# Layer 2: attention scores and their tanh moved into the step that makes their operand, next to the aggregation products

## The chip, the cores and the metric

The kernel runs on one core of one Trainium2 chip. A core has five engines that work side by side and wait for each other through semaphores: TensorE (PE, matrix products, written into the eight 2 KB PSUM banks of each partition), VectorE (DVE), ScalarE (ACT), GpSimd (POOL) and SyncE (SP, which only issues transfers here). The metric is the device time of one launch in microseconds (us). The kernel before takes 1876.17 us, the median of three runs from 1875.2 to 1877.63 us.

## The reference

128 graphs of 64 nodes, 256 features each, go through four layers of the form x + layer(relu(layernorm(x))). The change touches the third, called layer 2, a graph attention with 4 heads and a gate. For one graph with h the normalised input:

```python
Wh = einsum('bni,hoi->bhno', h, W) + bW          # 4 heads, 256 features each
e = einsum('bhno,hop->bhnp', Wh, attn)
scores = einsum('bhnp,bhmp->bhnm', e, Wh)
A_mat = tanh(where(adj, scores, 0.0))
hp = relu(einsum('bhnm,bhmo->bhno', A_mat, Wh))
ha = cat_of_heads(hp) @ A_w.T
hf = h @ fc_w.T
coeff = sigmoid(hf @ g1_w.T + ha @ g2_w.T + gbias)
return hf * coeff + ha * (1.0 - coeff)
```

## The kernel before

The tokens are cut into 32 groups of 256 (four graphs, held as two pairs of 128 partitions). A layer is a software pipeline over groups, written out by hand for every engine as one function `step(g)`; `run_steps` calls it for g = 0 to 34, the middle ones in a loop of two. In step g of layer 2 an engine works on several groups at once: `gn` = g is being normalised, `b1` = g-1 gets its dense products, `c2` = g-2 its attention, and `e` = g-3 its final blend and store. Nothing reorders instructions: each engine takes them as `step` writes them. `after(engine, signal, group, k)` is a wait, `known(...)` is one that is emitted only outside the loop, because inside another wait implies it.

The weights are folded so that the scores of a head need one dense product: **G** (`product_g(h)`, 12 matmuls of 128x256 for each of 4 heads, each in three parts because operands are split in a high and a low half, `mm3`, L188 to L190) gives `gT`, written out of PSUM with a bias by VectorE (L1789). The **scores** are then `gT` against the transposed input `ln.hT` (L1968, 32 small products for a group; the trace lists 64). A row term is added as the bias of the **tanh** on ScalarE (L1743, result `th`), and it comes from four extra columns of **Wh**, the last four of 1028 (`WC`). Wh (`product_wh(i)`) is made in six units `UNITS = (pair, first column, width)`; VectorE writes each to `wh` (L1799). Two units, those that begin at column 768, are 260 wide and hold the four bias columns.

`th` times the adjacency matrix is `a`, the heads 0 and 1 by GpSimd (L1713) and 2 and 3 by VectorE (L1832). The **hp** products (L1937, the trace lists 128 small matmuls) multiply `a` with `wh`; ScalarE takes the relu (L1733, `cat_hi`), VectorE the low half (L1806, `cat_lo`). Then come the `ha` products with `aw` (96 matmuls), `hf` and the gate products with `sq`. After the gate product ScalarE takes a tanh (L1771), VectorE blends in three operations (`diff` L1814, `part` L1817, `yT` L1822), TensorE transposes `yT` into bank 0 (L1982) and VectorE adds the residual to give `y` (L1844).

TensorE's order in a step before: scores of c2; G products of heads 0 and 1 of b1; transposes of `yT` of e; G products 2 and 3; hp of c2; six Wh units of b1; transposes of the normalised input of gn (L307, bank 0); `ha`; `hf`; gate. The scores use bank 4, the G products banks 1, 2, 3 and 1.

VectorE's order in a step before: `diff`, `part`, `yT` of e; layernorm statistics (L262); `a` of c2; the rest of the statistics (L269, L274); `gT` 0 and 1; `y`; `gT` 2 and 3; `ln_shift` (L288); three `cat_lo`, `wh` unit 0, the fourth `cat_lo`, the other `wh` units; then the low halves of the next operands.

Of the kernel before, what the change touches and what calls it, by code (L numbers as in the profile page):

```python
# [16 lines left out]
P = 128  # L17
S = 64
D = 256
KC = D // P  # L20
PAIRS = 2
# [75 lines left out]
def known(eng, signal, g, k=None, apart=None):  # L97

    if g.reg is None:
        after(eng, signal, g, k, apart)
# [1496 lines left out]
def graph_attention_layer(core, ln, x_dram, y_dram, adjT, weights, loaded_early, next_weights):  # L1600
# [6 lines left out]
    H = 4  # L1607
    CH = H * KC
    WC = H * D + H
    UNITS = ((0, 0, 512), (1, 0, 512), (0, 512, 256), (0, 768, WC - 768), (1, 512, 256), (1, 768, WC - 768))  # L1610
    graph_attention_setup(core, weights, loaded_early, next_weights)
    ctx = ExitStack()
    with ctx:  # L1613
# [39 lines left out]
                          "blend_steps", "proj_in_psum", "y_ready"]  # L1653
        B_HT = B_YT = 0
        B_G, B_WH, B_HF = (1, 2, 3, 1), (2, 3, 1, 2, 3, 1), 2
        B_GATE, B_S = 3, 4
        B_HP, B_HA = ((5, 6), (4, 7)), (7, 5)
        HEADS_OF_POOL, HEADS_OF_DVE = slice(0, 2), slice(2, H)
        halves = lambda bank: ps[:, bank, :].rearrange("p (c t) -> p c t", c=KC)
# [5 lines left out]
        def first_products(g):  # L1665


            return g.reg is None and g.c == 1
# [56 lines left out]
        @block.scalar  # L1725
        def _(act):
            def step(g):
                gn = ln.group(g)
                c2, b1 = g.back(2), g.back(1)

                def round_hp(i):
                    after(act, hp_in_psum, c2, i + 1)
                    nc.scalar.activation(in_cat(cat_hi, i), of_two_heads(i), ACT.Relu).then_inc(cat_hi_ready.sem, 1)  # L1733

                if c2.exists(groups):
                    known(act, a_pool_ready, c2.back(1))
                    known(act, a_dve_ready, c2.back(1))
                    after(act, wh_ready, c2)
                    after(act, scores_in_psum, c2)
                    for h in range(H):  # L1740
                        for p in range(PAIRS):
                            col = (p * H + h) * S
                            last = nc.scalar.activation(th[:, p, h], ps[:, B_S, col:col + S], ACT.Tanh,  # L1743
                                                        bias=wh[:, p, H * D + h:H * D + h + 1], scale=1.0)
                    last.then_inc(th_ready.sem, 1)
                if c2.exists(groups):
                    known(act, ha_in_psum, c2.back(1))
                    for i in range(H):
                        round_hp(i)
                if gn is not None:  # L1750
                    ln.apply(act, gn)
                if gn is not None:
                    known(act, scores_in_psum, gn.back(2))
                    ln.evacuate_hi(act, gn, B_HT)
                if c2.exists(groups):
                    known(act, gate_in_psum, c2.back(1))
                    for c in range(KC):
                        after(act, ha_in_psum, c2, c + 1)
                        nc.scalar.activation(ha_hi[:, c], ha(c), ACT.Copy).then_inc(ha_hi_ready.sem, 1)
                if b1.exists(groups):  # L1760
                    after(act, hf_in_psum, b1)
                    known(act, gate_in_psum, b1.back(2))
                    known(act, blend_steps, b1.back(2), 1)
                    nc.scalar.activation(hf_hi[:, b1.slot], halves(B_HF), ACT.Copy)
                    nc.scalar.activation(hf[:, b1.slot], halves(B_HF), ACT.Copy).then_inc(hf_hi_ready.sem, 1)
                if c2.exists(groups):

                    after(act, gate_in_psum, c2)
                    known(act, blend_steps, c2.back(1), 2)
                    for c in range(KC):  # L1770
                        last = nc.scalar.activation(gate[:, c], ps[:, B_GATE, c * TOK:(c + 1) * TOK], ACT.Tanh,  # L1771
                                                    bias=half_gbias[:, c:c + 1], scale=0.5)
                    last.then_inc(gate_ready.sem, 1)
                if first_products(g):
                    next_weights.split_hi(act)

            run_steps(act, step, groups, 2)

        @block.vector
        def _(dve):  # L1780
            def step(g):
# [10 lines left out]
                def evacuate_wh(i):  # L1792
                    p, c0, n = UNITS[i]
                    after(dve, wh_in_psum, b1, i + 1)
                    if i == 0:
                        known(dve, hp_in_psum, b1.back(1), 2)
                    if i == 2:
                        known(dve, hp_in_psum, b1.back(1))
                    nc.vector.tensor_tensor(wh[:, p, c0:c0 + n], ps[:, B_WH[i], 0:n], wh_bias[:, c0:c0 + n],  # L1799
                                            ALU.add).then_inc(wh_ready.sem, 1)  # L1800

# [81 lines left out]
        def _(pe):  # L1883
            def step(g):
# [35 lines left out]
                def product_hp():  # L1920
# [7 lines left out]
                    for h in range(H):  # L1928
# [10 lines left out]
                        if h % 2 == 1:  # L1939
                            for b in range(2):  # L1940
                                last[b].then_inc(hp_in_psum.sem, 1)

                def product_wh(i):
                    p, c0, n = UNITS[i]

# [7 lines left out]
                                       lambda t: t[:, c, p * P:(p + 1) * P], lambda t: t[:, c, c0 + k:c0 + k + w])  # L1953
                    last.then_inc(wh_in_psum.sem, 1)

                if c2.exists(groups):
                    u = c2.slot
                    known(pe, g_ready, c2, apart=core)
                    if first_products(g.back(1)):
                        pe.wait_ge(next_weights.made.sem, next_weights.SMALL_MADE)  # L1960
                    known(pe, th_ready, c2.back(1), apart=core)
                    for p in range(PAIRS):
                        for h in range(H):
                            col = (p * H + h) * S
                            for c in range(KC):
                                for b in range(2):
                                    toks = slice(p * P + b * S, p * P + (b + 1) * S)
                                    last = nc.tensor.matmul(ps[b * S:(b + 1) * S, B_S, col:col + S], gT[:, h, c, toks],  # L1968
                                                            ln.hT[:, u, c, toks], start=c == 0, stop=c == KC - 1,
                                                            skip_group_check=True)  # L1970
                    last.then_inc(scores_in_psum.sem, 1)
                if b1.exists(groups):
                    known(pe, ln.hT_hi_ready, b1)
                    after(pe, ln.hT_lo_ready, b1)
# [10 lines left out]
                if b1.exists(groups):  # L1985
                    product_g(2)
                    product_g(3)
                if c2.exists(groups):
                    known(pe, wh_ready, c2)
                    after(pe, a_dve_ready, c2, apart=core)  # L1990
                    after(pe, a_pool_ready, c2, apart=core)
                    product_hp()
                if b1.exists(groups):
                    for i in range(6):
                        product_wh(i)
                if gn is not None:
                    known(pe, y_ready, gn.back(3))
                    ln.transpose(pe, gn, B_HT)
                if c2.exists(groups):
                    after(pe, cat_lo_ready, c2)  # L2000
# [201 lines left out]
```

## Time and profile before

| | |
|---|---|
| median of 3 runs | 1876.17 us |
| profiled execution, its own time | 1874.63 us |
| its span | 1872.8 us |
| PE busy | 1813.7 us (97% of the span) |
| DVE busy | 1270.2 us (68%) |
| ACT busy | 896.9 us (48%) |
| POOL busy | 683.9 us (37%) |
| first and last score product of layer 2 | 676.9 us and 1479.8 us |

A timeline row gives the start and the duration in us, the engine, the line of the program, the operation, the tiles (written <- read), the shapes and how many instructions are merged in the row; in brackets the idle time before it and what ended it. Matmuls overlap: one of 128x256 lasts 0.28 us in the trace, and the next starts 0.11 us after it. PEclk is the granted TensorE clock as a share of full speed (2.4 GHz; 0.5 is 1.2 GHz).

### The profile page before, as it was taken

Reading aid. Unit: us, or ns where it says so; the run is one execution under the profiler, and the core shown is the slowest. Engines: PE = TensorE matmul, PEld = TensorE weight load, DVE = VectorE, ACT = ScalarE, POOL = GpSimd, SP = SyncE. Lnnn points to the kernel's source line nnn. Section 1 sums busy time; section 2 is a strip of 40 time slices with the busy share of each in tenths; the row PEclk is TensorE's granted clock in tenths of the full one; section 3 lists DMA queues with packets and bytes.
Section 4 is the critical chain, followed back from the end, with each engine's and each line's share of the span. In section 5 each row is a group of like instructions: output and inputs, shape, how many; then the busy total and the mean of one; then the engine's idle time right before and its main releaser. Section 6 shows DMA issues by size and latency. Waiting matters only on the chain. (4 is left out here: it accounts for less than half of the span.)

```text
span 1872.8 us, 74709 instructions
## 1 busy us (share of the span) xinstructions
PE 1813.7 (97%) x31152; PEld 1728.8 (92%) x31152; DVE 1270.2 (68%) x2887; ACT 896.9 (48%) x1997; POOL 683.9 (37%) x872
## 2 busy tenths in 40 slices
PE   7999999799999899999999999999999889999997
PEld 7899999699999799999999999999999889999997
DVE  6777777577777545555555555565555569999997
ACT  6777777566666523333333333333333335555554
POOL 3556665334343200000000000000000068999897
PEclk9999999999999999999999999999999999999999
DMA  3323223353333211101111011110111012222222
GB/s 109 88 74 86 81 73 86 111 151 91 97 91 98 89 30 37 35 26 29 34 34 34 23 29 34 34 34 23 34 29 34 19 48 78 69 69 80 74 69 64
DMA packets 149460, 113.66 MB, mean 61 GB/s; under 512 B 43009, under 2 KB 148865, under 8 KB 149377
## 3 DMA queue, kind: packets, MB, share of 16 engines
q1 hardware_dynamic: 149376, 112.46, 20.6%
q8 instruction: 63, 1.03, 0.2%
q14 instruction: 21, 0.16, 0.0%
HBM read 78.87 MB, written 33.55 MB: 60 GB/s over the span
## 5 line engine op out<-in xcount | busy, mean ns | idle before, releaser
L281 POOL TENSOR_TENSOR ln_rstd<-ln_var_eps,minus_half 128x2 f32<-128x2 f32 x128 | 91.1, 712 | 937.0 <-DVE ln_var_eps L274 934.4
L188 PE MATMUL banks<-ln_hT_hi,square_w_hi_held 128*128 128x256 f32 x512 | 149.5, 292 | 3.9 <-DVE square_w_lo_held L663 3.2
L188 PE MATMUL banks<-ln_hT_hi,l_g_w_hi 128*128 128x256 f32 x512 | 148.5, 290 | 2.1 <-PEq L2032 2.1
L299 ACT ACTIVATE ln_h<-ln_x,ln_shift,ln_rstd 128x256 f32<-128x256 f32 x256 | 140.0, 601 | 19.5 <-DVE ln_shift L288 17.8
L1733 ACT ACTIVATE l_cat_hi<-banks 128x512 fp32r<-128x512 f32 x128 | 66.3, 603 | 172.9 <-PE banks L1937 172.9
L188 PE MATMUL banks<-l_wh_w_hi,ln_hT_hi 128*128 128x256 f32 (+1 forms) x512 | 145.2, 284 | 0.0
L188 PE MATMUL banks<-l_cat_hi,l_aw_hi 128*128 128x256 f32 x512 | 144.9, 283 | 0.0
L189 PE MATMUL banks<-ln_hT_lo,square_w_hi_held 128*128 128x256 f32 x512 | 143.5, 280 | 0.0
L190 PE MATMUL banks<-ln_hT_hi,square_w_lo_held 128*128 128x256 f32 x512 | 143.4, 280 | 0.0
L190 PE MATMUL banks<-l_wh_w_hi,ln_hT_lo 128*128 128x256 f32 (+1 forms) x512 | 142.5, 278 | 0.0
L190 PE MATMUL banks<-ln_hT_hi,l_g_w_lo 128*128 128x256 f32 x512 | 142.4, 278 | 0.0
L189 PE MATMUL banks<-l_wh_w_lo,ln_hT_hi 128*128 128x256 f32 (+1 forms) x512 | 142.2, 278 | 0.0
L189 PE MATMUL banks<-ln_hT_lo,l_g_w_hi 128*128 128x256 f32 x512 | 142.2, 278 | 0.0
L189 PE MATMUL banks<-l_cat_lo,l_aw_hi 128*128 128x256 f32 x512 | 142.0, 277 | 0.0
L190 PE MATMUL banks<-l_cat_hi,l_aw_lo 128*128 128x256 f32 x512 | 141.9, 277 | 0.0
L322 DVE TENSOR_TENSOR ln_hT_lo<-banks,ln_hT_hi 128x512 fp32r<-128x512 f32 x128 | 88.5, 691 | 73.9 <-ACT ln_hT_hi L317 72.8
L528 POOL TENSOR_TENSOR l_weighted<-l_prob,l_rz 128x512 f32<-128x512 f32 x96 | 100.2, 1044 | 67.1 <-DVE l_rz L710 63.1
L188 PE MATMUL banks<-square_w_hi_moved,ln_hT_hi 128*128 128x256 f32 x384 | 117.3, 305 | 2.5 <-PEq L1613 1.9
L1799 DVE TENSOR_TENSOR l_wh<-banks,l_wh_bias 128x256 f32<-128x256 f32 (+1 forms) x192 | 98.5, 515 | 30.5 <-PE banks L190 28.3
L1789 DVE TENSOR_TENSOR l_gT<-banks,l_v_col 128x512 f32<-128x512 f32 x128 | 85.6, 689 | 36.9 <-PE banks L190 36.9
L190 PE MATMUL banks<-square_w_hi_moved,ln_hT_lo 128*128 128x256 f32 x384 | 107.9, 281 | 0.0
L189 PE MATMUL banks<-square_w_lo_moved,ln_hT_hi 128*128 128x256 f32 x384 | 107.7, 280 | 0.0
(222 smaller groups left out, 6312.8 us busy)
## 6 DMA issues: line engine op xcount, KB each, us to landing
hidden<-y SPq DMA_DIRECT2D x96, 256.0 KB, 2.1
ln_x<-hidden SPq DMA_DIRECT2D x96, 256.0 KB, 2.8
x_res<-hidden SPq DMA_DIRECT2D x96, 256.0 KB, 2.9
ln_x<-x SPq DMA_DIRECT2D x32, 256.0 KB, 2.8
x_res<-x SPq DMA_DIRECT2D x32, 256.0 KB, 3.0
out<-y SPq DMA_DIRECT2D x32, 256.0 KB, 2.1
l_adj_u<-adj SPq DMA_DIRECT2D x96, 16.0 KB, 2.3
l_stage_attn<-L_attn SPq DMA_DIRECT2D x4, 256.0 KB, 3.3
```

The lines of the kernel that those rows point to most:

```text
L188: nc.tensor.matmul(out, lhs(lh), rhs(rh), start=start, stop=False, skip_group_check=True)
L189: nc.tensor.matmul(out, lhs(lh), rhs(rl), start=False, stop=False, skip_group_check=True)
L190: return nc.tensor.matmul(out, lhs(ll), rhs(rh), start=False, stop=stop, skip_group_check=True)
L281: self.nc.gpsimd.tensor_tensor(self.rstd[:, g.slot], self.var_eps[:, g.slot], self.core.minus_half[:, 0:PAIRS], ALU.pow).then_inc(self.rst ...
L299: last = self.nc.scalar.activation(self.h[:, u, p, :], self.x[:, u, p, :], ACT.Relu, bias=self.shift[:, u, p:p + 1], scale=self.rstd[:, u, ...
L322: self.nc.vector.tensor_tensor(self.hT_lo[:, u], self.core.ps[:, bank, :].rearrange("p (c t) -> p c t", c=KC), self.hT_hi[:, u], ALU.subtr ...
L528: nc.gpsimd.tensor_tensor(weighted[:, c2.slot, t], prob[:, c2.slot, t], rz[:, c2.slot, t].unsqueeze(2).to_broadcast([P, ROWS_OF_TILE, S]), ...
L1733: nc.scalar.activation(in_cat(cat_hi, i), of_two_heads(i), ACT.Relu).then_inc(cat_hi_ready.sem, 1)
L1789: nc.vector.tensor_tensor(gT[:, h], halves(B_G[h]), v_col[:, h].unsqueeze(2).to_broadcast([P, KC, TOK]), ALU.add).then_inc(g_ready.sem, 1)
L1799: nc.vector.tensor_tensor(wh[:, p, c0:c0 + n], ps[:, B_WH[i], 0:n], wh_bias[:, c0:c0 + n], ALU.add).then_inc(wh_ready.sem, 1)
```

## The change

The scores of group b1 are now computed in the same step as its G products, right behind the hp products of group c2. Their tanh is taken in that step too, behind the normalisation of gn on ScalarE. The two units of Wh with the bias columns go first; the first stands ahead of hp, the second behind the scores. The scores use bank 0, between the transposes of `yT` and those of the normalised input, which now wait for the tanh. In front of hp stands a new wait for all four `gT` of b1. The parts of the diff:

```diff
-    UNITS = ((0, 0, 512), (1, 0, 512), (0, 512, 256), (0, 768, WC - 768), (1, 512, 256), (1, 768, WC - 768))
+    UNITS = ((0, 768, WC - 768), (1, 768, WC - 768), (0, 0, 512), (1, 0, 512), (0, 512, 256), (1, 512, 256))
-        B_GATE, B_S = 3, 4
+        B_GATE, B_S = 3, 0
@@ ScalarE
                 if c2.exists(groups):
-                    known(act, a_pool_ready, c2.back(1))
-                    known(act, a_dve_ready, c2.back(1))
-                    after(act, wh_ready, c2)
-                    after(act, scores_in_psum, c2)
+                    known(act, ha_in_psum, c2.back(1))
+                    for i in range(H):
+                        round_hp(i)
+                if gn is not None:
+                    ln.apply(act, gn)
+                if b1.exists(groups):
+                    known(act, a_pool_ready, b1.back(1))
+                    known(act, a_dve_ready, b1.back(1))
+                    after(act, wh_ready, b1, 2)
+                    after(act, scores_in_psum, b1)
                     for h in range(H):
...
-                if c2.exists(groups):
-                    known(act, ha_in_psum, c2.back(1))
-                    for i in range(H):
-                        round_hp(i)
-                if gn is not None:
-                    ln.apply(act, gn)
@@ VectorE, evacuate_wh
                     if i == 0:
-                        known(dve, hp_in_psum, b1.back(1), 2)
-                    if i == 2:
-                        known(dve, hp_in_psum, b1.back(1))
+                        after(dve, hp_in_psum, b1.back(1))
@@ TensorE
-                if c2.exists(groups):
-                    u = c2.slot
-                    known(pe, g_ready, c2, apart=core)
...
+                def scores():
+
+                    u = b1.slot
+                    known(pe, y_ready, e)
@@ TensorE, order of the step
                 if b1.exists(groups):
                     product_g(2)
                     product_g(3)
+                    product_wh(0)
+                    after(pe, g_ready, b1, apart=core)
                 if c2.exists(groups):
                     known(pe, wh_ready, c2)
                     after(pe, a_dve_ready, c2, apart=core)
                     after(pe, a_pool_ready, c2, apart=core)
                     product_hp()
                 if b1.exists(groups):
-                    for i in range(6):
+                    scores()
+                    for i in range(1, 6):
                         product_wh(i)
                 if gn is not None:
-                    known(pe, y_ready, gn.back(3))
+                    after(pe, th_ready, b1)
                     ln.transpose(pe, gn, B_HT)
```

What this does to the instructions, first on TensorE where a step begins, inside the loop: the end of the gate product, and what follows it, up to the transposes of `yT`. Before:

```order
L190 MATMUL banks<-l_ha_hi,l_sq_lo 128x256
L126 UNCONDITIONAL_BRANCH
L1968 MATMUL banks<-ln_hT,l_gT 64x64 x32
L90 ISA
L188 MATMUL banks<-ln_hT_hi,l_g_w_hi 128x256 [waits hT_lo_ready]
...
L1982 MATMUL banks<-constants_sb,l_yT 128x128 [waits blend_steps]
```

After, at the same place:

```order
L190 MATMUL banks<-l_ha_hi,l_sq_lo 128x256
L126 UNCONDITIONAL_BRANCH
L126 ISA
L188 MATMUL banks<-ln_hT_hi,l_g_w_hi 128x256 [waits hT_lo_ready]
...
L1979 MATMUL banks<-constants_sb,l_yT 128x128 [waits blend_steps]
```

The 32 score products are gone from between the gate product and the G products; 24 matmuls of G (the dots) now stand alone between the gate product and the transposes that wait for the blend.

The second place is TensorE around hp (L1937 before, L1935 after), with the last G product ahead of it. Before:

```order
L190 MATMUL banks<-ln_hT_hi,l_g_w_lo 128x256
L1937 MATMUL banks<-l_a,l_wh 64x64 [waits a_dve_ready,a_pool_ready]
L1937 MATMUL banks<-l_a,l_wh 64x64 x63
L90 REGISTER_ALU
L188 MATMUL banks<-l_wh_w_hi,ln_hT_hi 128x256 [waits g_ready]
```

After:

```order
L190 MATMUL banks<-ln_hT_hi,l_g_w_lo 128x256
L90 REGISTER_ALU
L188 MATMUL banks<-l_wh_w_hi,ln_hT_hi 128x260 [waits g_ready]
...
L190 MATMUL banks<-l_wh_w_hi,ln_hT_lo 128x260
L1935 MATMUL banks<-l_a,l_wh 64x64 [waits g_ready,a_dve_ready,a_pool_ready]
L1935 MATMUL banks<-l_a,l_wh 64x64 x63
L1951 MATMUL banks<-ln_hT,l_gT 64x64 x32
L90 REGISTER_ALU
L188 MATMUL banks<-l_wh_w_hi,ln_hT_hi 128x260 [waits g_ready]
```

Six matmuls of the first Wh unit moved ahead of hp, hp also waits for `g_ready` (the four `gT` written by VectorE), and the scores stand behind hp with no big product between them.

The third place is ScalarE, from the relu of hp to the copies of the transposed input. Before:

```order
L1743 ACTIVATE l_th<-banks,l_wh 128x64 x7
L90 ISA
L1733 ACTIVATE l_cat_hi<-banks 128x8x64 [waits hp_in_psum]
...
L299 ACTIVATE ln_h<-ln_x,ln_shift,ln_rstd 128x256 [waits ln_shift_ready]
L299 ACTIVATE ln_h<-ln_x,ln_shift,ln_rstd 128x256
L316 ACTIVATE ln_hT<-banks 128x512 [waits hT_in_psum]
```

After:

```order
L1733 ACTIVATE l_cat_hi<-banks 128x8x64 [waits hp_in_psum]
...
L299 ACTIVATE ln_h<-ln_x,ln_shift,ln_rstd 128x256
L90 ISA
L90 REGISTER_ALU [waits wh_ready]
L1749 ACTIVATE l_th<-banks,l_wh 128x64 [waits scores_in_psum_of_1]
L1749 ACTIVATE l_th<-banks,l_wh 128x64 x7
L316 ACTIVATE ln_hT<-banks 128x512 [waits hT_in_psum]
```

The tanh moved from ahead of the relu of hp to behind the normalisation. The order of VectorE's kinds of work, and all of GpSimd and SyncE, stay as they were; on VectorE only the widths of the six `wh` writes change places.

## Rows read from the trace of the kernel before

**Rows 1.** Windows view: start and end, length, busy time by engine, PEclk, DMA

```profile
340.00:640.00 300.00, 286.66 (x4084) 262.21 (x4083) 200.19 (x487) 177.29 (x343) 109.39 (x132) 0.99 0.36 105
1000.00:1250.00 250.00, 250.00 (x3618) 246.31 (x3618) 139.89 (x300) 82.68 (x214) 17.54 (x27) 1.00 0.11 31
```

**Rows 2.** Timeline of PE over one step, and the start of the next

```profile
909.16 2.08 PE L1968 MATMUL banks<-ln_hT,l_gT 128*64 128x64 f32 x64
911.18 0.38 PE L188 MATMUL banks<-ln_hT_hi,l_g_w_hi 128*128 128x256 f32 x1
911.40 0.28 PE L189 MATMUL banks<-ln_hT_lo,l_g_w_hi 128*128 128x256 f32 x1
...
914.03 0.60 PE L1982 MATMUL banks<-constants_sb,l_yT 128*128 128x128 f32 x4
...
917.29 2.10 PE L1937 MATMUL banks<-l_a,l_wh 64*64 64x64 f32 x128
919.31 0.38 PE L188 MATMUL banks<-l_wh_w_hi,ln_hT_hi 128*128 128x256 f32 x1
...
922.82 0.28 PE L188 MATMUL banks<-l_wh_w_hi,ln_hT_hi 128*128 128x260 f32 x1
...
923.54 0.28 PE L188 MATMUL banks<-l_wh_w_hi,ln_hT_hi 128*128 128x256 f32 x1
...
924.94 0.60 PE L307 MATMUL banks<-constants_sb,ln_h 128*128 128x128 f32 x4
...
935.01 0.80 PE L1968 MATMUL banks<-ln_hT,l_gT 128*64 128x64 f32 x20
```

**Rows 3.** Timeline of ACT over the same step

```profile
909.27 0.84 ACT L1771 ACTIVATE l_gate<-banks,l_half_gbias 128x256 f32<-128x256 f32 x2 [1.63 <-PE banks L190]
911.29 1.75 ACT L1743 ACTIVATE l_th<-banks,l_wh 128x64 f32<-128x64 f32 x8 [1.19 <-PE banks L1968]
918.50 2.07 ACT L1733 ACTIVATE l_cat_hi<-banks 128x512 fp32r<-128x512 f32 x4 [5.45 <-PE banks L1937]
920.43 1.11 ACT L299 ACTIVATE ln_h<-ln_x,ln_shift,ln_rstd 128x256 f32<-128x256 f32 x2
```

**Rows 4.** Timeline of DVE over the same step

```profile
910.14 0.75 DVE L1814 TENSOR_TENSOR l_diff<-l_hf,banks 128x256 f32<-128x256 f32 x2 [1.78 <-ACT l_gate L1771]
...
911.66 0.75 DVE L1822 SCALAR_TENSOR_TENSOR l_yT<-l_part,banks 128x256 f32<-128x256 f32 x2
912.33 0.75 DVE L262 BATCH_NORM_STATS2 ln_stats<-ln_x 128x6 f32<-128x256 f32 x2
913.08 0.42 DVE L1832 TENSOR_TENSOR l_a<-l_th,l_adj 128x256 f32<-128x256 f32 x1
...
913.80 1.29 DVE L1789 TENSOR_TENSOR l_gT<-banks,l_v_col 128x512 f32<-128x512 f32 x2
915.00 0.68 DVE L1844 TENSOR_TENSOR y<-banks,x_res 128x512 f32<-128x512 f32 x1
...
917.40 0.69 DVE L1789 TENSOR_TENSOR l_gT<-banks,l_v_col 128x512 f32<-128x512 f32 x1 [0.67 <-PE banks L190]
918.00 0.15 DVE L288 SCALAR_TENSOR_TENSOR ln_shift<-ln_mean_var,ln_rstd 128x2 f32<-128x2 f32 x1
```

**Rows 5.** Timeline of POOL over the same step

```profile
914.64 0.74 POOL L1713 TENSOR_TENSOR l_a<-l_th,l_adj 128x256 f32<-128x256 f32 x1
```

**Rows 6.** Timeline of DVE in step 33, near the layer's end

```profile
1480.42 0.75 DVE L1822 SCALAR_TENSOR_TENSOR l_yT<-l_part,banks 128x256 f32<-128x256 f32 x2
```

**Rows 7.** Timeline of PE in step 33, three places

```profile
1481.23 0.65 PE L1982 MATMUL banks<-constants_sb,l_yT 128*128 128x128 f32 x4 [1.21 <-DVE l_yT L1822]
...
1484.48 2.85 PE L1937 MATMUL banks<-l_a,l_wh 64*64 64x64 f32 x128 [2.60 <-issue]
...
1490.65 0.41 PE L189 MATMUL banks<-l_cat_lo,l_aw_hi 128*128 128x256 f32 x1
1490.87 0.41 PE L190 MATMUL banks<-l_cat_hi,l_aw_lo 128*128 128x256 f32 x1
```

More of the change, by code:

```diff
@@ L1941, in product_hp @@
                                 last[b].then_inc(hp_in_psum.sem, 1)
+                def scores():
+                    u = b1.slot
+                    known(pe, y_ready, e)
+                    for p in range(PAIRS):
+                        for h in range(H):
+                            col = (p * H + h) * S
+                            for c in range(KC):
+                                for b in range(2):
+                                    toks = slice(p * P + b * S, p * P + (b + 1) * S)
+                                    last = nc.tensor.matmul(ps[b * S:(b + 1) * S, B_S, col:col + S], gT[:, h, c, toks],
+                                                            ln.hT[:, u, c, toks], start=c == 0, stop=c == KC - 1,
+                                                            skip_group_check=True)
+                    last.then_inc(scores_in_psum.sem, 1)
                 def product_wh(i):
@@ L1954, in product_wh @@
                     last.then_inc(wh_in_psum.sem, 1)
-                if c2.exists(groups):
-                    u = c2.slot
-                    known(pe, g_ready, c2, apart=core)
[L1959 to L1971, printed above, removed]
                 if b1.exists(groups):
```

## The prediction, on record before the result

> **What bounds the kernel now.** I read the windows view first, then one step of layer 2 engine by engine in the timeline, then the layer's end. In the windows view the reader is to see that TensorE has no idle time in layer 2: 250.00 us busy of 250.00, at full clock, while VectorE is busy 139.89 and ScalarE 82.68 [rows 1]. So a step costs what TensorE's list of instructions costs, and an edit can only gain by making that list shorter or lose by putting a wait into it. In TensorE's timeline one step goes from the scores at 909.16 to the scores at 935.01, 25.85 us [rows 2]. The other engines' rows show how much room each of TensorE's waits has, and that is what the change spends: it takes no product away, it only moves 2 us of them.
>
> **What the order saves.** Every change between big and small matmuls costs a little. The first big one behind the scores starts at 911.18 and the second at 911.40, 0.22 apart, where the pitch elsewhere is 0.11; going in costs about as much. A block of small ones thus costs some 0.2 us beside its own time. Today a step has two such blocks, scores (909.16 to 911.18, 2.02) and hp (917.29 to 919.31, 2.02) [rows 2]. Behind the change they touch, and one pair of switches goes: up to 0.2 us in each of 32 steps. The trace has no hp block directly followed by scores, so the joint costs between 0 and 0.1; I take 0.05, since both are small fp32 products.
>
> **The cover that goes: the blend of e.** At the step's start the scores stand between the gate product and the G products. While they run, ScalarE takes the gate's tanh (from 909.27) [rows 3] and VectorE does diff, part and yT, which end at 911.66 + 0.75 = 912.41 [rows 4]. TensorE comes to the transposes of yT at 914.03 [rows 2], 1.6 us late enough. Nothing in this chain depends on the scores: it starts with the end of the gate product and keeps its times. Without the 2.02 us of scores and their entry and exit (0.2), TensorE does G 0 and 1 from 909.05 and is at the transposes at about 914.03 - 2.1 = 911.9. yT is ready at 912.41, and the start follows by 0.06: in step 33 yT ends at 1480.42 + 0.75 = 1481.17 and the transposes start at 1481.23 [rows 6, 7]. TensorE now waits until 912.47, about 0.55 us, in each step that has an e and a b1.
>
> **The second wait: four gT before hp.** VectorE goes on in its fixed order: statistics, a, the rest of the statistics, gT 0 and 1 from 913.80, y from 915.00, then gT 2 and 3. Before, it was idle 0.67 us ahead of gT 3 [rows 4], since TensorE was the later one. Now TensorE is earlier and VectorE is not. The pitch of its 512-wide operations is 0.60 (gT 3 at 917.40, the next at 918.00) [rows 4], so gT 2 starts at 915.60, gT 3 at 916.20 and ends at 916.89. The operation a no longer waits for the tanh, which ended at 911.29 + 1.75 = 913.04 [rows 3]; that returns at most 0.08 us, so 916.81 to 916.89. TensorE after its transposes at 912.47 needs 3.26 us for them and G 2 and 3 (914.03 to 917.29) and 0.72 for the first Wh unit (922.82 to 923.54) [rows 2]: it is at hp at 916.45. G 3 also needs bank 1 back, that is gT 0, written by about 914.45, where TensorE arrives at 914.3; this lies inside the same wait. So hp waits for gT 3, until 916.9 or 917.0. I take 0.06 for the way of the semaphore and 0.08 for the freed a in half: 916.92. At the other end stands the 0.2 us of hp in step 33, where a of GpSimd was the last to come: 917.1. GpSimd's a, which ended at 914.64 + 0.74 = 915.38 before [rows 5], hangs on VectorE's statistics and keeps that time; it isn't last.
>
> At this wait a rule of the Trainium skill makes another sum. gT 3 ends by the row at 918.09, and ln_shift starts at 918.00, ahead of that end [rows 4]. "VectorE: DVE Perf Modes", section "The DRAIN you can't avoid", says that the next operation does not start until the pipe is empty. By that rule gT 0 to gT 3 would stand a whole duration apart, about 0.3 us more in a step and 9 us in all. The row shows the earlier start, and the sum goes by the row.
>
> **Sum of a step.** From one hp to the next TensorE runs without a wait except these. The step loses or gains: hp starts at 916.92 instead of 917.29 (-0.37), the scores follow (+2.02, joint +0.05), the first Wh unit is already done (-0.72). That is +0.98 us. The ends: -0.45 + 2.02 + 0 - 0.72 = +0.85, and -0.19 + 2.02 + 0.1 - 0.72 = +1.21. As a check from the waits: 0.55 + 0.5 of idle time less 0.2 for a pair of switches, with the joint back, is +0.9.
>
> **Sum of the layer.** Steps 3 to 32 have both e and b1: 30 x 0.98 = 29.4 us (25.5 to 36.3). Step 2 has no blend; there hp waits only for gT 3: gT 3 is written 1.0 behind the start of the last G matmul (0.28 + 0.69) and the Wh unit covers 0.83 of it (0.11 + 0.72), so it loses 0.2 and gains 0.2. Step 1 did no scores before and does them now: 2.02 + 0.2 for the switches + 0.2 of wait = +2.4. Step 33 no longer has scores, but there TensorE stood still for GpSimd's a anyway, 2.60 us [rows 7], and that comes from the gate by way of VectorE's statistics; it gets 0.1 faster. The layer is 29.4 + 2.4 - 0.1 = +31.7 us (27.8 to 38.6) longer.
>
> **Edits I cost at nothing.** The tanh now stands behind the relu of hp and the normalisation. Those end 4.3 us behind the start of hp (920.43 + 1.11 against 917.29) [rows 2, 3]. The scores end 4.1 behind hp, the second Wh unit (0.72) and its write (0.4) are through at about 5.6, the tanh takes 1.75: 7.4. TensorE reaches the transposes of gn at 4.1 + 0.1 + (924.94 - 919.31) - 0.72 = 9.1 behind hp. Cover 1.7 us; were it gone, each step would pay the difference. Queued behind the tanh on ScalarE are the copies of those transposes, which could not start sooner. The VectorE writes of Wh get two narrow ones first; each bank is free over 1 us before its next unit. The wait for hp in front of `wh` unit 0 follows three `cat_lo` that needed hp already. No DMA moves, and GpSimd and SyncE keep their order.
>
> **To the measured time.** The profiled execution took 1874.63 us; with 31.7 it is 1906.3. The median of the runs shown is 1.5 above it, so I forecast 1908.
>
> **Rivals.**
> 1. Only the first wait appears (6%): VectorE catches up, hp never waits for gT 3. Then a step gains 0.15 of joined switches and pays 0.55: +0.4, 30 x 0.4 + 2.4 = +14, 1890. Against it: VectorE's operations from 910.14 to gT 3 leave no idle time to close.
> 2. The change is faster (4%): the switches saved are worth more than the waits. This decides at the transposes of yT: if yT were there by 911.9, which is 0.5 before its row, and VectorE's writes likewise, 32 x 0.2 = 6.4 would be gained and 2.4 paid in step 1: -4, 1872. The row of yT stands against it, as it hangs only on the gate product.
> 3. No measurable difference (3%): half of that shortening, 1877.
> 4. The small gaps, with the waits at two places in each step, cost clock (4%). At 1.2 GHz the pitch is 1490.87 - 1490.65 = 0.22 instead of 0.11 [rows 7], in a stretch that followed idle times of up to 2.6 us. If some 13 matmuls a step ran so, +1.4 more, 30 x 1.4 = 42: 1950. Against it, layer 1 leaves TensorE 13 us idle of 300 and keeps 0.99 of the clock [rows 1]. "TensorE: Matmul & The Clock Gate" of the Trainium skill, section "A second HAM failure mode: psum-queue depth-cycling", speaks for this rival: frequent micro-idles between groups made the clock oscillate there. The trace of layer 1 does not agree with it.
> 5. The tanh is late for the transposes of gn (3%): the cover of 1.7 is used up and 0.5 more: 30 x 0.5 = 15, 1923.
>
> **How the numbers follow.** The forecast, both waits at about their sizes, has 80%. Its own range is 1904 to 1915. About 0.2% (3.7 us) can be told from no change. Faster has 4% (rival 2), same 3% (rival 3), slower 93%. The range 1897 to 1917 holds the forecast with room for a joint or a wait smaller than bounded, and leaves out rivals 1 to 5.
>
> **What would show it.** In the profile after: TensorE idle ahead of the transposes of yT, released by VectorE's yT, 0.5 to 0.6 us, 30 times; TensorE idle ahead of hp, released by VectorE's gT, 0.4 to 0.6 us, about as often; a step of 26.8 us from one hp to the next; scores 2.0 us behind the start of hp; VectorE without idle time from diff to gT 3; no wait of TensorE for the tanh; PEclk still 1.0 in the middle of the layer. I am wrong if hp starts without a wait, if VectorE's chain from the gate to gT 3 is shorter than 7.5 us, or if the step is under 26.3 us.

## The result, and the profile after

| | before | after |
|---|---|---|
| median | 1875.68 us (4 runs) | 1916.05 us (4 runs, 1911.57 to 1916.11) |
| ratio after/before | | 1.0215, 95% interval 1.0202 to 1.0228 |
| profiled execution, span | 1872.8 us | 1914.3 us |
| step of layer 2 inside the loop, from gate's tanh to gate's tanh, mean of 26 | 25.85 us | 27.17 us |

The change makes the kernel slower by 40.4 us. The forecast was 1908 with a range from 1897 to 1917: the direction and both waits were right, the size was 8 us short. Most of that is one term of the sum, how long hp takes to start behind the gT it waits for; the rest is the clock at the layer's end.

The windows view of the kernel after (columns as in [rows 1]) over the same stretch of time:

```profile
1000.00:1250.00 250.00, 240.75 (x3464) 234.83 (x3463) 132.61 (x291) 77.89 (x200) 17.56 (x27) 1.00 0.10 29
```

Where TensorE had no idle time it now stands still for 9.3 of 250 us. Its clock is still 1.00, so it isn't slower work but waiting. The waits view over the middle of the layer (700 to 1470 us) says for whom; its columns are the engine and line that waited, what for, the total in us, how often and the longest:

```profile
PE banks L1979 <- DVE l_yT L1820: 14.8, 29, 0.5
PE banks L1935 <- DVE l_gT L1789: 11.5, 25, 0.5
```

These are the two waits of the prediction, at the transposes of yT (L1979) and at hp (L1935), and the view lists no third. The timeline of TensorE over a step inside the loop, to be held against [rows 2]:

```profile
921.89 0.28 PE L190 MATMUL banks<-ln_hT_hi,l_g_w_lo 128*128 128x256 f32 x1
922.67 0.66 PE L1979 MATMUL banks<-constants_sb,l_yT 128*128 128x128 f32 x4 [0.51 <-DVE l_yT L1820]
923.08 0.36 PE L188 MATMUL banks<-ln_hT_hi,l_g_w_hi 128*128 128x256 f32 x1
...
924.64 0.38 PE L188 MATMUL banks<-ln_hT_hi,l_g_w_hi 128*128 128x256 f32 x1
...
927.46 2.10 PE L1935 MATMUL banks<-l_a,l_wh 64*64 64x64 f32 x128 [0.46 <-DVE l_gT L1789]
929.49 2.09 PE L1951 MATMUL banks<-ln_hT,l_gT 128*64 128x64 f32 x64
931.50 0.39 PE L188 MATMUL banks<-l_wh_w_hi,ln_hT_hi 128*128 128x260 f32 x1
```

The timelines of ScalarE and VectorE over the same step, to be held against [rows 3, 4]:

```profile
919.48 0.84 ACT L1771 ACTIVATE l_gate<-banks,l_half_gbias 128x256 f32<-128x256 f32 x2 [1.63 <-PE banks L190]
```

```profile
921.86 0.75 DVE L1820 SCALAR_TENSOR_TENSOR l_yT<-l_part,banks 128x256 f32<-128x256 f32 x2
922.53 0.75 DVE L262 BATCH_NORM_STATS2 ln_stats<-ln_x 128x6 f32<-128x256 f32 x2
923.20 0.41 DVE L1830 TENSOR_TENSOR l_a<-l_th,l_adj 128x256 f32<-128x256 f32 x1
...
923.89 1.29 DVE L1789 TENSOR_TENSOR l_gT<-banks,l_v_col 128x512 f32<-128x512 f32 x2
925.10 0.68 DVE L1842 TENSOR_TENSOR y<-banks,x_res 128x512 f32<-128x512 f32 x1
925.70 1.32 DVE L1789 TENSOR_TENSOR l_gT<-banks,l_v_col 128x512 f32<-128x512 f32 x2
```

Take every time from the gate's tanh (919.48 here, 909.27 in the rows of before). yT ends at 3.13 (3.14 before), and the transposes start 0.06 later, at 3.19, with 0.51 us of idle time: all as forecast. (What the wait costs is more than this idle time: the matmul ahead of it started at 921.89, so 0.78 us lie between two starts that are 0.12 apart without a wait, 0.66 more.) gT 3 ends at 925.70 + 1.32 = 927.02, that is 7.54; the forecast had 7.54 to 7.62. But hp starts at 7.98, not at 7.65: 0.44 us pass between the end of what it waited for and its first matmul. That is the term that was too small. The same operation outside the loop, in the written-out step 4 of the kernel after, in the timelines of VectorE and TensorE:

```profile
762.83 1.33 DVE L1789 TENSOR_TENSOR l_gT<-banks,l_v_col 128x512 f32<-128x512 f32 x2
```

```profile
764.21 2.09 PE L1935 MATMUL banks<-l_a,l_wh 64*64 64x64 f32 x128
```

Here gT 3 ends at 764.16 and hp starts at 764.21, 0.05 behind. The written-out steps 3 to 5 and 32 take 26.71 to 26.89 us, where the forecast said 26.83 for every step; the 26 steps inside the loop take 27.17 on average.

### The profile page after: what moved, and what is told of

It is laid out like the page before. It is cut to its first block and busy times, and to the rows that moved or that the text cites. A ratio compares the mean times of both kernels' runs of the same rounds, so it can differ in the third digit from the quotient of the medians.

```text
span 1914.3 us, 74769 instructions
## 1 busy us (share of the span) xinstructions
PE 1825.4 (95%) x31152; PEld 1733.0 (91%) x31152; DVE 1261.7 (66%) x2887; ACT 896.0 (47%) x1997; POOL 684.0 (36%) x872
## 5 line engine op out<-in xcount | busy, mean ns | idle before, releaser
L1797 DVE TENSOR_TENSOR l_wh<-banks,l_wh_bias 128x260 f32<-128x260 f32 (+2 forms) x192 | 98.3, 513 | 76.6 <-PE banks L190 76.4
L1804 DVE SCALAR_TENSOR_TENSOR l_cat_lo<-banks,l_cat_hi 128x512 fp32r<-128x512 f32 x128 | 82.1, 683 | 70.2 <-ACT l_cat_hi L1733 70.2
```

The lines of the kernel that those rows point to most:

```text
L1804: nc.vector.scalar_tensor_tensor(out=in_cat(cat_lo, i), in0=of_two_heads(i), scalar=0.0, in1=in_cat(cat_hi, i), op0=ALU.max, op1=ALU.subtr ...
```

## The experiments

The question left by the result is where the 0.44 us comes from. Theory A: in the loop the wait for gT (`after(pe, g_ready, b1)`) is followed by two more waits for a, and each wait there is an instruction of its own that compares with a register's value and also increments a counter (`sem_inc`, L92). As long as TensorE's queue runs ahead of the array this costs nothing. When the queue is held at the first of them, what stands behind it is worked through in the open. Theory B: a wait for VectorE that ends late costs 0.44 by itself. The second question is what the moved scores cost once no wait is left. All "step" figures are means over the 26 steps inside the loop of the distance between two tanh of the gate, and a "gap" is the time from the end of gT 3 to the first matmul of hp; each ratio is to runs of the kernel before on the same chip.

**The wait for gT put last of the three (x1_gready_last)**

```diff
-                    after(pe, g_ready, b1, apart=core)
                 if c2.exists(groups):
                     known(pe, wh_ready, c2)
                     after(pe, a_dve_ready, c2, apart=core)
                     after(pe, a_pool_ready, c2, apart=core)
+                    if b1.exists(groups):
+                        after(pe, g_ready, b1, apart=core)
                     product_hp()
```

> The changed kernel, with the new wait for gT moved to be the last of the three in front of hp (behind those for the two halves of a). In the changed kernel hp starts 0.44 us behind the end of gT 3. Theory A: the wait itself is short, and the 0.44 is mostly TensorE's queue working through the two further waits and their counters once it is released; then hp starts about 0.2 us behind gT 3, a step is 26.9 us instead of 27.14, and the time is 1909 (-7). Theory B: any wait of hp for VectorE that ends late costs the 0.44; then nothing changes, step 27.14, 1916.

Measured: 1908.5 us, ratio 1.0175 (1.0147 to 1.0204), step 26.89. In the timeline of VectorE and of TensorE the gap is down to 0.15 (1029.81 + 1.32 = 1031.13 to 1031.28):

```profile
1029.81 1.32 DVE L1789 TENSOR_TENSOR l_gT<-banks,l_v_col 128x512 f32<-128x512 f32 x2
```

```profile
1031.28 2.10 PE L1935 MATMUL banks<-l_a,l_wh 64*64 64x64 f32 x128 [0.16 <-DVE l_gT L1789]
```

This is theory A: the step is 0.28 us shorter than in the changed kernel. (The 95% intervals of the two ratios, 1.0147 to 1.0204 here and 1.0202 to 1.0228 for the change, just touch; the steps tell the kernels apart better than the times.)

Only in the loop, though. In the written-out steps of this kernel the built program has the wait for gT ahead of those for a after all, as an instruction of its own, and there the gap is 0.36 (760.93 + 1.32 = 762.25 to 762.61), where the changed kernel had 0.05:

```profile
760.93 1.32 DVE L1789 TENSOR_TENSOR l_gT<-banks,l_v_col 128x512 f32<-128x512 f32 x2
```

```profile
762.61 2.10 PE L1935 MATMUL banks<-l_a,l_wh 64*64 64x64 f32 x128 [0.37 <-DVE l_gT L1789]
```

These four steps take 27.02 to 27.19 us, up to 0.44 longer than in the changed kernel. So written-out code isn't free of this cost; what decides is which wait the built program puts where. That each engine takes its instructions as `step` writes them holds for the work, not for the waits.

**The two waits for a written twice (x7_two_more_waits)**

```diff
                     after(pe, a_dve_ready, c2, apart=core)
                     after(pe, a_pool_ready, c2, apart=core)
+                    after(pe, a_dve_ready, c2, apart=core)
+                    after(pe, a_pool_ready, c2, apart=core)
```

> The changed kernel with the two waits for a in front of hp written twice, each with its counter, all behind the wait for gT. Both are long fulfilled. Theory A: each further wait with its counter costs about 0.15 us of TensorE's queue once it has been held, so hp starts 0.74 us behind gT 3 instead of 0.44, step 27.45, time 1925. Rival: a fulfilled wait is free and the 0.3 between the two orders had another reason; then nothing changes, 1916.

Measured: 1924.1 us, ratio 1.0263 (1.0248 to 1.0278), step 27.47. VectorE's and TensorE's timelines:

```profile
1010.01 1.30 DVE L1789 TENSOR_TENSOR l_gT<-banks,l_v_col 128x512 f32<-128x512 f32 x2
```

```profile
1012.07 2.10 PE L1935 MATMUL banks<-l_a,l_wh 64*64 64x64 f32 x128 [0.77 <-DVE l_gT L1789]
```

The gap is 0.76 us. With none, two and four fulfilled waits behind the late one it is 0.15, 0.44 and 0.76: about 0.15 us for each wait with its counter. The written-out steps stay at 26.72 to 26.89 us with the doubled waits. That is no test of a wait without a counter: there the built program puts the wait for gT last, on the first weight load of hp, and the waits for a are all passed over 1.2 us before gT 3 ends.

**Only the last counter kept (x10_one_counter)**

```diff
-                    after(pe, g_ready, b1, apart=core)
+                    after(pe, g_ready, b1)
...
-                    after(pe, a_dve_ready, c2, apart=core)
+                    after(pe, a_dve_ready, c2)
```

> The changed kernel with the same three waits in the same order in front of hp, but only the last of them followed by its counter (the other two counters left out; nothing reads them). If it is the counters (semaphore increments by TensorE's queue) that cost the time behind the release, hp starts about 0.2 us behind gT 3 instead of 0.44, step 26.9, time 1909. If it is the waits on a register's value themselves, it stays near 0.44 and the step at 27.14, time 1915. In between, each has its share.

Measured: 1908.86 us, ratio 1.0177 (1.0153 to 1.0201), step 26.88. The gap is 0.15 again:

```profile
1010.47 1.30 DVE L1789 TENSOR_TENSOR l_gT<-banks,l_v_col 128x512 f32<-128x512 f32 x2
```

```profile
1011.92 2.10 PE L1935 MATMUL banks<-l_a,l_wh 64*64 64x64 f32 x128 [0.16 <-DVE l_gT L1789]
```

The edit did not do what it was meant to do, so it doesn't separate the wait from its counter. Without the counters between them the built program passes the wait for a_pool early, during G 3, and joins those for gT and a_dve into one instruction with one counter: nothing stands behind the late one. Its gap of 0.15 is that of x1, and says no more than that fewer instructions cost less.

What a wait costs without a counter is shown by the written-out steps of x1. The trace also records the wait instructions of TensorE's queue, which the views leave out. In all these kernels the one for gT starts 0.04 us behind the end of gT 3, and hp's first matmul starts 0.11 behind the last wait instruction. Between two of them, once the first was late, pass 0.15 us where each has a counter and compares with a register (0.18 at times in x7), and 0.11 where they have no counter and compare with constants:

| steps | wait instructions from gT's on | gap |
|---|---|---|
| changed kernel, written out | none, the wait is on the weight load | 0.05 |
| x1 and x10, loop | 1 with its counter | 0.15 |
| x1, written out | 3 without counters | 0.36 |
| changed kernel, loop | 3 with counters | 0.45 |
| x7, loop | 5 with counters | 0.75 to 0.78 |

Each gap is the sum of these pieces: 0.04 + 2 x 0.15 + 0.11 = 0.45 in the loop of the changed kernel (the rounded rows gave 0.44), 0.04 + 2 x 0.11 + 0.11 = 0.36 or 0.37 in x1. So most of the 0.15 is the separate wait instruction, and about 0.04 the counter and the register together. No register instruction stands between the waits. A loop with separate waits and no counter at all wasn't run.

**The kernel before with the second wait alone (x6_before_with_wait)**

```diff
-    UNITS = ((0, 0, 512), (1, 0, 512), (0, 512, 256), (0, 768, WC - 768), (1, 512, 256), (1, 768, WC - 768))
+    UNITS = ((0, 768, WC - 768), (1, 768, WC - 768), (0, 0, 512), (1, 0, 512), (0, 512, 256), (1, 512, 256))
...
                     product_g(3)
+                    product_wh(0)
+                    after(pe, g_ready, b1, apart=core)
                 if c2.exists(groups):
...
-                    for i in range(6):
+                    for i in range(1, 6):
                         product_wh(i)
```

> The kernel before (scores at the head of the step, bank 4), with only the second part of the change: the bias units of Wh first, one of them ahead of hp, and hp waiting for all gT. TensorE comes to hp 0.72 us later than gT 3's product ends and gT 3 is written about 1.0 behind that product's start. Theory A (a wait placed ahead of the two waits for a costs 0.44 behind its release): hp starts 0.5 us later than without a wait, step 26.35 us, time 1890 to 1892. Rival (the release costs 0.06 to 0.1): step 25.95, time 1878 to 1879.

Measured: 1891.51 us, ratio 1.0092 (1.0077 to 1.0107), step 26.42. The scores stand where they stood and VectorE is idle ahead of gT 3 as before; TensorE's row:

```profile
1029.54 2.09 PE L1935 MATMUL banks<-l_a,l_wh 64*64 64x64 f32 x128 [0.46 <-DVE l_gT L1789]
```

So the wait in front of hp is a cost of its own, 17 us, also where the blend isn't late. A first Wh unit of 0.72 us doesn't cover gT 3, and the wait adds its 0.44.

**The wait for gT behind hp (x2_gready_behind_hp)**

```diff
-                    after(pe, g_ready, b1, apart=core)
...
                 if b1.exists(groups):
+                    after(pe, g_ready, b1, apart=core)
                     scores()
```

> The changed kernel, with the wait for gT moved from in front of hp to between hp and the scores, which are what reads gT. Theory A: gT 3 ends 0.1 us after TensorE could begin hp, so the wait is over long before the scores and costs nothing; hp starts without idle time, about 7.45 us behind the gate's tanh instead of 7.98, step 26.6 us, time 1900 (-16). Rival: a wait of TensorE's queue costs its 0.4 us wherever it stands (the queue has to stop for it), then the idle time moves to the front of the scores and the time stays at 1914 to 1916.

Measured: 1897.19 us, ratio 1.012 (1.0095 to 1.0145), step 26.60. Only the scores read gT, and in front of them the same wait is over before TensorE's array gets there. TensorE over one step (the gate's tanh at 1019.20):

```profile
1021.60 0.28 PE L190 MATMUL banks<-ln_hT_hi,l_g_w_lo 128*128 128x256 f32 x1
1022.39 0.66 PE L1979 MATMUL banks<-constants_sb,l_yT 128*128 128x128 f32 x4 [0.51 <-DVE l_yT L1820]
...
1026.65 2.10 PE L1935 MATMUL banks<-l_a,l_wh 64*64 64x64 f32 x128
1028.68 2.09 PE L1951 MATMUL banks<-ln_hT,l_gT 128*64 128x64 f32 x64
```

hp starts at 7.45 without idle time, and the scores follow 2.03 later without idle time. The wait for yT is the only one left.

**The transposes of yT behind G 2 (x3_yt_behind_g2)**

```diff
                 if b1.exists(groups):
                     product_g(2)
+                if e.exists(groups):
+                    after(pe, blend_steps, e)
...
+                if b1.exists(groups):
                     product_g(3)
```

> The changed kernel, with the transposes of yT moved behind the G products of head 2. Theory A: VectorE's row of operations from the gate's tanh to gT 3 sets the start of hp, so the 0.5 us wait at the transposes vanishes and comes back in front of G 3 (which needs bank 1 back from gT 0) and hp; hp stays about 8.0 us behind the gate's tanh, step 27.1 us, time 1914 to 1916. Rival: the two waits are separate costs; then the first goes, the step is 26.6 us and the time 1900.

Measured: 1914.55 us, ratio 1.0205 (1.018 to 1.023), step 27.22. The waits view of this kernel (700 to 1470 us):

```profile
PE banks L188 <- DVE l_gT L1789: 19.6, 29, 0.7
PE banks L1935 <- DVE l_gT L1789: 11.6, 25, 0.5
```

The wait for yT went and came back at G 3, which needs bank 1 from gT 0. It is one row of VectorE's operations, from the gate's tanh to gT 3, that TensorE runs into, wherever it first meets it.

**The same with the wait for gT behind hp (x12_behind_hp_yt_late)**

> The changed kernel with the wait for gT behind hp and the transposes of yT behind the G products of head 2, but VectorE's order left alone. Theory A: VectorE's row of operations behind the gate's tanh still brings gT 0 only 5.1 us behind that tanh, so TensorE waits 0.7 us in front of G 3 for bank 1: step 26.5 to 26.6 us, time 1896. Rival: with both places of waiting removed nothing is left to wait for; step 25.7, time 1872.

Both edits above, together. Measured: 1897.93 us, ratio 1.0131 (1.0104 to 1.0158), step 26.61, with one wait left (waits view, 700 to 1440 us):

```profile
PE banks L188 <- DVE l_gT L1789: 19.0, 28, 0.7
```

**VectorE's statistics and a ahead of the blend (x4_dve_early)**

```diff
+                if gn is not None:
+                    ln.statistics(dve, gn, first=True)
+                if c2.exists(groups):
...
+                if gn is not None:
+                    ln.statistics(dve, gn, first=False)
                 if e.exists(groups):

                     after(dve, gate_ready, e)
```

> The changed kernel, with VectorE's statistics and its half of a moved in front of the blend, where VectorE waits 1.8 us for the gate's tanh. Theory A: yT is not earlier, so the wait at the transposes stays 0.5 us; gT 0 is 1.3 us earlier, so G 3 no longer waits for bank 1 (0.1 to 0.2 us), and gT 3 is then bound by its product: it ends some 0.8 us behind the last G 3 matmul, and hp follows 0.44 later; hp about 7.8 us behind the gate's tanh, step 26.95, time 1910. Rival: the row of VectorE operations is all of the second wait; then it goes and the time is 1900.

Measured: 1912.31 us, ratio 1.0194 (1.0167 to 1.0221), step 27.14. gT 3 is now bound by its product, G 3 no longer waits for bank 1, and the 0.46 us in front of hp stay. The step is 0.19 us longer than the 26.95 expected, and the gain on the changed kernel isn't clear of noise. One row differs from the expectation. The timelines of VectorE and GpSimd:

```profile
1001.70 0.75 DVE L1824 TENSOR_TENSOR l_diff<-l_hf,banks 128x256 f32<-128x256 f32 x2 [0.45 <-ACT l_gate L1771]
1002.48 0.84 DVE L1827 SCALAR_TENSOR_TENSOR l_part<-l_gate,l_diff 128x512 f32<-128x512 f32 x1
```

```profile
1002.03 0.74 POOL L1713 TENSOR_TENSOR l_a<-l_th,l_adj 128x256 f32<-128x256 f32 x1
1002.75 0.98 POOL L1720 TENSOR_SCALAR l_adj<-l_adj_u 128x128 f32<-128x128 uint8 x1
```

GpSimd's work starts earlier too and now runs beside the blend. `part` takes 0.84 us instead of 0.69, and GpSimd's conversion of the mask 0.98 instead of 0.53, so yT is 0.15 later and the wait at the transposes 0.66. `diff` and `yT`, which read PSUM, keep their 0.75; `part` is the one with both inputs in SBUF. "GPSIMD Engine Reference" of the Trainium skill, in its section "1. Specifications", names this case, contention for the shared SBUF interfaces with VectorE operations that have two SBUF inputs; the rows agree.

**That with the wait for gT behind hp (x9_behind_hp_dve_early)**

> As the first, but with the transposes of yT left behind G 1, so only the first wait remains. Theory A: TensorE waits 0.65 us for yT (the blend's second operation was 0.15 longer with VectorE's early work), nothing else; step 26.4 to 26.6 us, time 1889 to 1896, and the difference to the first kernel is the price of the cover that went. Rival: the wait is taken up elsewhere and the time is as that of the first.

"The first" in this text is the kernel of the next paragraph. Measured: 1898.01 us, ratio 1.0125 (1.011 to 1.014), step 26.60, with 0.66 us of waiting at the transposes of yT and none else. The time is 2 us above the upper end of what was expected. It is 28 us above the kernel of the next paragraph, which is the price of the cover that went.

**All three together (x5_all)**

> The changed kernel with all three mendings: the wait for gT behind hp, the transposes of yT behind the G products of head 2, and VectorE's statistics and a ahead of the blend. Theory A (the loss is nothing but TensorE's waits, plus the slower pitch of the matmuls right behind a wait): no wait is left in the step, hp about 6.6 us behind the gate's tanh, one pair of switches between big and small products saved, step 25.65 to 25.75 us against 25.85 of the kernel before; step 1 costs 2.4, the end of the layer gains about 3 since a of the last group no longer waits for the blend; time 1869 to 1873, at or just under the kernel before. Rival (the joined small products or the narrow Wh units ahead cost something themselves): step 25.9 to 26.0, time 1877 to 1880.

Measured: 1869.96 us (12 runs), ratio 0.9973 (0.9963 to 0.9982), step 25.65. In the middle of the layer TensorE's waits view is empty, as before the change. Its timeline over a step (the gate's tanh at 1013.44):

```profile
1017.32 0.60 PE L1981 MATMUL banks<-constants_sb,l_yT 128*128 128x128 f32 x4
1017.68 0.37 PE L188 MATMUL banks<-ln_hT_hi,l_g_w_hi 128*128 128x256 f32 x1
...
1019.95 2.10 PE L1935 MATMUL banks<-l_a,l_wh 64*64 64x64 f32 x128
1021.97 2.09 PE L1951 MATMUL banks<-ln_hT,l_gT 128*64 128x64 f32 x64
1023.99 0.39 PE L188 MATMUL banks<-l_wh_w_hi,ln_hT_hi 128*128 128x260 f32 x1
```

hp at 6.51 behind the gate's tanh, no idle time, and the step is 0.20 us shorter than before: the one pair of switches that the prediction gave to the joined blocks, with the joint between hp and the scores (2.02 after the start of hp) at zero. The end of the layer gained less than the 3 us expected: hp of step 33 starts 2.5 us sooner behind the gate's tanh than before, but the step takes 22.03 us instead of 22.97. This version is faster than the kernel before by 4 us, 0.27%, in runs side by side, and faster than the changed kernel, which ran apart from it, by some 46 us.

## Why the prediction was right, and where it was short

1. **TensorE bounds the layer, and only waits or switches change the step.** Right. The windows view fell from 250.00 to 240.75 busy, and with all waits taken away the step is 25.65.
2. **The cover of the blend goes: 0.55 us at the transposes of yT.** Right: 0.51 of idle time, start at 3.19 behind the gate's tanh. With this wait as the only one the step is 26.60 (x2), against 25.65 without (x5). The delayed start is 0.66 of these 0.95 us. The prediction had 0.55 because it let TensorE arrive 0.1 later than it could; the transposes themselves started when it said.
3. **VectorE's row ends with gT 3 at 7.54 to 7.62.** Right: 7.54. The pitch of 0.60 held (0.62 at gT 3), and a came 0.09 sooner than before. The prediction's other sum, by "VectorE: DVE Perf Modes" of the Trainium skill, section "The DRAIN you can't avoid", would have put gT 3 some 0.3 later. It left out that the same section lets an operation that isn't held start earlier, and these rows do.
4. **hp starts 0.06 behind it.** This is the step that was mis-sized, at its "0.06 for the way of the semaphore". In the written-out steps it is 0.05; in the loop it is 0.45, because there the wait for gT is an instruction of its own (0.15 instead of 0.05) and two more, at 0.15 each, stand behind it. The row of step 33, the far end of the bound at 0.2, was taken from written-out code. The loop's steps take 27.17 instead of 26.83, some 8.7 us more in 26 steps. Most of this is the 0.33 by which hp starts later than forecast. Several of the steps are also 0.15 longer than the others, in the spacing of the Wh products; why is open.
5. **The joint of hp and scores, 0.05.** It is 0.00 (hp to scores 2.02 or 2.03 in all timelines above). x5, with no wait left, is 0.20 shorter than before.
6. **Step 1 costs 2.4.** From the first G product to the first tanh of the gate the layer takes 48.99 us instead of 46.38, 2.6 more.
7. **Step 33 gains 0.1.** hp came 0.2 sooner (6.22 behind the gate's tanh, 6.44 before), but the step is 25.23 instead of 22.97. The scores are no longer there, so TensorE stands still 3.23 us, and then 2.38 before hp. In the timeline of the kernel after:

```profile
1519.88 0.66 PE L1979 MATMUL banks<-constants_sb,l_yT 128*128 128x128 f32 x4 [3.23 <-DVE l_yT L1820]
1522.91 3.69 PE L1935 MATMUL banks<-l_a,l_wh 64*64 64x64 f32 x128 [2.38 <-issue]
1528.85 1.09 PE L307 MATMUL banks<-constants_sb,ln_h 128*128 128x128 f32 x4 [2.24 <-ACT ln_h L299]
...
1534.43 0.41 PE L189 MATMUL banks<-l_cat_lo,l_aw_hi 128*128 128x256 f32 x1
1534.64 0.41 PE L190 MATMUL banks<-l_cat_hi,l_aw_lo 128*128 128x256 f32 x1
```

   hp takes 3.69 us instead of 2.85 [rows 7], and matmuls at the 1.2 GHz pitch, 0.21, go on for 6.0 us behind the start of those transposes (until 1534.86), where before it was 2.8 us. That it is the clock is shown by x12, whose step 33 has the same order on TensorE and waits of 3.23, 2.22 and 2.24 us. The windows view over step 33, of the kernel before, the changed kernel and x12:

```profile
1478.00:1501.00 23.00, 15.91 (x273) 15.04 (x272) 9.03 (x20) 7.10 (x19) 1.42 (x2) 0.85 0.04 13
```

```profile
1516.70:1541.90 25.20, 16.36 (x208) 15.62 (x208) 8.94 (x20) 5.33 (x11) 1.42 (x2) 0.73 0.03 12
```

```profile
1497.40:1519.70 22.30, 13.54 (x208) 12.68 (x208) 8.94 (x20) 5.38 (x12) 1.42 (x2) 0.85 0.04 13
```

   With the same work at a mean clock of 0.85 instead of 0.73 the step takes 22.25 us instead of 25.23. So the clock, priced as a rival for the step, came at this one place, and how much of it came is in part chance: over six kernels with this same order in step 33 (the changed one, x1, x2, x3, x10, x12) it takes 22.25 to 25.23 us.
8. **What was costed at nothing.** The tanh wasn't waited for in any step, and the DMA share of the windows view is 0.10, 0.11 before.

The sum of the profile: 2.6 for the start, 38.1 for steps 3 to 32 (25.85 x 30 = 775.6 before, 813.7 after) and 2.3 for step 33 are 43.0, where the forecast had 2.4, 29.4 and -0.1, that is 31.7. Of the 11.3 between them 8.7 are in steps 3 to 32, above all the late start of hp, and 2.4 in step 33. The spans differ by only 41.5, since layer 2 began 2.0 earlier in this execution than in the other and what follows it took 0.5 longer, which belongs to other layers. And the forecast added 1.5 from the profiled execution to the median, which in the kernel after are the same. That is why the number was only 8 us short: part of the error was cancelled by luck.

Of the rivals, the clock in every step is excluded by PEclk 1.00, the single wait by the waits view. The late tanh did not show.

## What to carry to other kernels

When a block of work is moved off the bounding engine's path, ask first what it covered: the scores were not only 2 us of TensorE but also the time in which VectorE made yT, and three orders on two engines had to follow before the move paid. Put a wait as late as its first real reader, and behind every wait that is sure to be fulfilled; then look where the built program has it, for x1 and x10 show it moving and joining waits. A wait that is met early costs nothing; one that holds the queue also makes everything that stands behind it in the queue visible.

## What the runs showed of the hardware that wasn't expected

- A wait of TensorE that really holds costs about 0.15 us for each further wait instruction with a counter that stands behind it (gaps of 0.15, 0.45 and 0.75 us with none, two and four), and 0.11 us for each without a counter (0.36 with two, in the written-out steps of x1). On the first weight load of hp the same wait costs 0.05.
- Waits of 0.5 us at two places in every 27 us left the granted clock at 1.00. At the layer's end the idle times of 3.2 and 2.4 us, 0.7 us of work apart, were followed by hp at the slow pace (3.69 us), before the third idle time of 2.2 us; but how long the clock stayed at 1.2 GHz differed between kernels with nearly the same waits there.
- The idle time of the views understates what a wait costs, since a matmul lasts 0.28 us in the trace and the next starts 0.12 behind it. From x5 to x2 the step grows by 0.95 us with 0.51 idle. The starts say where it goes: 0.66 at the wait for yT (1021.60 to 1022.39 instead of 0.12), 0.06 in the transposes behind it, 0.23 in G 2 and G 3, most of that at the first two matmuls of G 3, which wait for bank 1 without an idle time that the view shows.
- A VectorE operation with two inputs in SBUF took 0.84 instead of 0.69 us beside GpSimd's work, and operations that read one input from PSUM did not change.
